# A two-layer graph network on Trainium2: comparisons on 2-byte operands, and another split between two passes

## What is computed

```
h = relu(layernorm(x))
agg = segment_sum(h[src] + edge_attr, dst)            # layer 0
x = x + batchnorm(relu(agg @ W1 + b1) @ W2 + b2)
h = relu(layernorm(x));  dis = rsqrt(degree)          # layer 1
h = relu(segment_sum((h @ W1)[src] * dis[src] * dis[dst], dst) + b1)
h = relu(segment_sum((h @ W2)[src] * dis[src] * dis[dst], dst) + b2)
x = x + (h - mean(h)) / sqrt(var(h) + eps) * ln_w + ln_b
```

## Time and profile before

| | |
|---|---|
| median of 3 runs | 2910.58 us (2907.73 to 2920.95) |
| profiled execution | 2908.32 us, span 2906.8 us |
| busy | PE 2552.8 us (88%), PEld 2416.9, DVE 1743.1 (60%), ACT 888.7, POOL 1993.7 (69%) |
| DMA | 503.37 MB, mean 173 GB/s |

### The profile page before, as it was taken

How to read it: one execution, slowest core, us unless ns; L and a number is a source line. 1 busy time by engine, 2 the same in 40 slices (tenths; PEclk the granted TensorE clock), 3 DMA queues, 4 the chain that set the end, 5 groups by cost and what they waited for, 6 DMA issues and landing times.

```text
span 2906.8 us, 64340 instructions
## 1 busy us (share of the span) xinstructions
PE 2552.8 (88%) x25984; PEld 2416.9 (83%) x25984; DVE 1743.1 (60%) x4148; ACT 888.7 (31%) x1492; POOL 1993.7 (69%) x1903
## 2 busy tenths in 40 slices
PE   0388988989888898895699999999997999999996
PEld 0277878878787787784699999999997999999996
DVE  8898999989988899895444444454430222222222
ACT  7344444444444444454522222232210000000001
POOL 6777777777777778710377777767706777777772
PEclk9899999999999999996799999999998999999998
DMA  4455565555556555543765555655557666666664
GB/s 116 118 149 144 147 171 151 155 157 153 148 160 153 150 148 168 148 125 105 231 204 201 163 200 196 211 181 179 200 186 203 221 206 214 208 213 199 199 214 131
DMA packets 341214, 503.37 MB, mean 173 GB/s; under 512 B 278659, under 2 KB 284217, under 8 KB 316082
## 3 DMA queue, kind: packets, MB, share of 16 engines
q1 hardware_dynamic: 280102, 402.60, 42.8%
q0 software_dynamic: 60192, 93.34, 14.0%
q10 hardware_dynamic: 616, 3.20, 0.4%
HBM read 361.86 MB, written 137.13 MB: 172 GB/s over the span
## 4 chain that ended last, share of the span: by engine, by line
PE 42%; POOL 37%; issue 11%; DVE 5%; DMA 2%; ACT 1%; SPq 1%; DVEq 0%; ACTq 0%; POOLq 0%
POOL arena L1273 37%; PE psum L1110 32%; PE psum L1089 3%; PE psum L1132 3%; PE psum L1071 1%; DMA arena<-table,srcT 1%; ACT arena L818 1%; DMA arena<-in_edge_attr_dram 1%; SPq L1288 0%; PE psum L1125 0%; PE psum L1195 0%; DMA arena<-table 0%; DVE arena L961 0%; DVE arena L834 0%; DVE arena L844 0%
## 5 line engine op out<-in xcount | busy, mean ns | idle before, releaser
L1273 POOL DMA_INDIRECT arena<-table,srcT x1840 | 1913.0, 1040 | 696.3 <-issue 626.5
L1110 PE MATMUL psum<-arena 125*125 125x193 bf16 (+1 forms) x19200 | 2009.1, 250 | 44.8 <-DMA arena<-counts 23.0
L1110 PEld LDWEIGHTS psum<-arena 125*125 125x125 fp8e4 x19200 | 1879.1, 140 | 87.1 <-DMA arena<-counts 23.5
L1211 ACT CAST arena<-psum 125x500 uint16<-125x500 f32 (+1 forms) x923 | 647.3, 711 | 1084.3 <-PE psum L1089 1079.8
L1089 PE MATMUL psum<-arena 128*125 128x300 f16 x1775 | 609.9, 346 | 31.6 <-DVE arena L961 24.5
L961 DVE TENSOR_SCALAR arena<-iota,keyT,oddT 128x300 f16<-128x300 f16 x1775 | 579.3, 353 | 1.4 <-PE psum L1089 1.3
L1089 PEld LDWEIGHTS psum<-arena 128*125 128x125 f16 x1775 | 247.8, 140 | 79.5 <-DVE arena L961 58.4
L971 DVE SCALAR_TENSOR_TENSOR arena<-relT,psum 128x960 bf16<-128x960 f16 x272 | 308.6, 1134 | 0.0
L987 DVE TENSOR_TENSOR arena<-arena 128x650 f32<-128x650 f32 (+1 forms) x334 | 272.8, 817 | 24.8 <-DMA arena<-in_edge_attr_dram 24.6
L958 DVE TENSOR_TENSOR arena<-modT,psum 128x625 f16<-128x625 f16 x355 | 281.0, 792 | 0.2 <-issue 0.2
L994 DVE TENSOR_REDUCE arena<-psum 96x65 f32<-96x195 f32 (+1 forms) x275 | 96.3, 350 | 307.4 <-PE psum L1132 303.4
(11 more groups left out here) (219 smaller groups left out, 954.2 us busy)
## 6 DMA issues: line engine op xcount, KB each, us to landing
arena<-counts SPq DMA_DIRECT2D x121, 1600.0 KB
counts<-arena SPq DMA_DIRECT2D x71, 1600.0 KB, 6.1
arena<-in_edge_attr_dram SPq DMA_DIRECT2D x166, 320.0 KB
arena<-table,srcT POOLq DMA_INDIRECT x1840
table<-arena SPq DMA_DIRECT2D x8, 1050.0 KB
table<-arena SPq DMA_DIRECT2D x25, 168.0 KB
arena<-table SPq DMA_DIRECT2D x4, 1050.0 KB
arena<-in_x_dram ACTq DMA_DIRECT2D x4, 700.0 KB
```

The source lines that it names most:

```text
L1110: last = pe.matmul(ps_v[n % 2][0:PN, 0:xc], A(slot)[0:PN, j, 0:PN], Xs[0:PN, j, 0:xc], start=(j == 0), stop=(j == J - 1))
L1211: act.copy(A2(slot)[0:PN, :, i // 2 * NWORD:i // 2 * NWORD + n_w], ps_b[at % NBANK][0:PN, :].rearrange("p (j x) -> p j x", x=NWORD)[:, :, ...
L1273: pool.indirect_dma_start(out=gbuf(slot)[0:parts, t, :], out_offset=None, in_=tables[k], in_offset=bass.IndirectOffsetOnAxis(ap=idx, axis= ...
```

## The change

Three things. First, `DENSE` becomes (62, 69, 69): pass 0 treats 62 windows as dense and builds 62 tiles, pass 1 builds 9 and loads 60; `QG[0]` goes from 88 to 102. Second, a table of the numbers as 2-byte floats is put in PSUM once, each number five times in a row, and the two comparisons read it; a mask is now made by two `tensor_tensor` operations on 480 columns each instead of one `scalar_tensor_tensor` on 960. Third, for that the layouts turn: `relT` and its source in DRAM have the 10 edges of a partition innermost, a mask has the 10 t of one slot adjacent (so the weights of one t are 96 elements with a step of 10), and `ob` has the 5 runs of one number adjacent (weights: 125 elements with a step of 5).

```diff
-DENSE = (54, 69, 69)
+DENSE = (62, 69, 69)
-        relT = sb("relT", [P, NT, G], F16)
+        relT = sb("relT", [P, G, NT], F16)
+        n_num = (PN * NB4 + 1) // 2
+        ps_n5 = psum[:, 2, P:P + n_num]
+        num_dn = ps_n5.bitcast(F16)[:, 0:PN * NB4].rearrange("p (d n) -> p d n", n=NB4)
         def ob(k):
-            return part(o_ob, k, n_ob).bitcast(F16)[:, 0:NB4 * PN].rearrange("p (n d) -> p n d", d=PN)
+            return part(o_ob, k, n_ob).bitcast(F16)[:, 0:NB4 * PN].rearrange("p (d n) -> p d n", n=NB4)
         def sbuf(n):
+            return part(o_S, n, NT * W // 2).bitcast(BF16).rearrange("p (w t) -> p w t", t=NT)
...
+            nums = arena[:, o_t + NE + 16:o_t + NE + 16 + n_num]
+            V(dve.memset(nums, 0.0))
+            V(dve.tensor_copy(nums.bitcast(F16)[:, 0:PN * NB4].rearrange("p (d n) -> p d n", n=NB4),
+                              iota[:, 0:PN].rearrange("p (d a) -> p d a", a=1).broadcast_to([P, PN, NB4])))
+            V(dve.tensor_copy(ps_n5, nums))
...
-                        mod = modT[:, v:v + NB4].rearrange("p (n a) -> p n a", a=1).broadcast_to([P, NB4, PN])
-                        it = ps_i[:, 0:PN].rearrange("p (a d) -> p a d", a=1).broadcast_to([P, NB4, PN])
-                        dve.tensor_tensor(ob(four % NOB), mod, it, ALU.is_equal)
+                        mod = modT[:, v:v + NB4].rearrange("p (a n) -> p a n", a=1).broadcast_to([P, PN, NB4])
+                        dve.tensor_tensor(ob(four % NOB), mod, num_dn, ALU.is_equal)
...
-                        rel = relT[:, :, g:g + 1].broadcast_to([P, NT, W])
-                        it = ps_i[:, 0:W].rearrange("p (a w) -> p a w", a=1).broadcast_to([P, NT, W])
-                        dve.scalar_tensor_tensor(out=S, in0=rel, scalar=0.0, in1=it, op0=ALU.add,
-                                                 op1=ALU.is_equal).then_inc(v_S, 1)
+                        for t0 in (0, NB4):
+                            rel = relT[:, g:g + 1, t0:t0 + NB4].broadcast_to([P, W, NB4])
+                            last = dve.tensor_tensor(S[:, :, t0:t0 + NB4], rel, num_dn[:, 0:W, :], ALU.is_equal)
+                        last.then_inc(v_S, 1)
...
-                    pe.matmul(to[:, :, 2 * side:2 * side + 3], ob(v // NB4 % NOB)[:, v % NB4, :],
+                    pe.matmul(to[:, :, 2 * side:2 * side + 3], ob(v // NB4 % NOB)[:, :, v % NB4],
...
-                            last = pe.matmul(ps_q, S[0:parts, t, :], e3(v % NEDGE)[0:parts, t, :, :],
+                            last = pe.matmul(ps_q, S[0:parts, :, t], e3(v % NEDGE)[0:parts, t, :, :],
```

More of the change, by code:

```diff
@@ L13 @@
 U16 = mybir.dt.uint16
-U8 = mybir.dt.uint8
 X = mybir.AxisListType.X
@@ L310, in bass_gnn_preln_kernel @@
         ps_i = psum[:, 2, 0:P]
+        n_num = (PN * NB4 + 1) // 2
+        ps_n5 = psum[:, 2, P:P + n_num]
+        num_dn = ps_n5.bitcast(F16)[:, 0:PN * NB4].rearrange("p (d n) -> p d n", n=NB4)
+        assert NT == 2 * NB4
         ps_t = [psum[:, i, :] for i in range(2)]
@@ L346, in sbuf, with sbuf_rows @@
         def sbuf(n):
+            return part(o_S, n, NT * W // 2).bitcast(BF16).rearrange("p (w t) -> p w t", t=NT)
+        def sbuf_rows(n):
             return part(o_S, n, NT * W // 2).bitcast(BF16).rearrange("p (t w) -> p t w", w=W)
@@ L514, in sp_load @@
             sp.dma_start(run_first, row_first).then_inc(l_first, 16)
-            sp.dma_start(dst_i, dst_turned.rearrange("p t g -> p (t g)")).then_inc(l_dst, 16)
+            sp.dma_start(dst_i, dst_turned.rearrange("p g t -> p (g t)")).then_inc(l_dst, 16)
             sp.dma_start(base_b, group_first.broadcast_to([P, NG])).then_inc(l_dst, 16)
@@ L728, in dve_lists @@
             dve.wait_ge(l_dst, 2 * 16)
-            firsts = base_b[:, 0:G].rearrange("p (a g) -> p a g", a=1).broadcast_to([P, NT, G])
-            dve.tensor_tensor(relT[:, :, :], dst_i.rearrange("p (t g) -> p t g", g=G), firsts, ALU.subtract).then_inc(
+            firsts = base_b[:, 0:G].rearrange("p (g a) -> p g a", a=1).broadcast_to([P, G, NT])
+            dve.tensor_tensor(relT[:, :, :], dst_i.rearrange("p (g t) -> p g t", t=NT), firsts, ALU.subtract).then_inc(
                 v_list, 1)
@@ L738, in dve_check_lists @@
         def dve_check_lists():
-            every = relT.rearrange("p t g -> p (t g)")
+            every = relT.rearrange("p g t -> p (g t)")
             dve.wait_ge(v_list, 2)
@@ L968, in dve_pass @@
                     if g < G:
-                        rel = relT[:, :, g:g + 1].broadcast_to([P, NT, W])
-                        it = ps_i[:, 0:W].rearrange("p (a w) -> p a w", a=1).broadcast_to([P, NT, W])
-                        dve.scalar_tensor_tensor(out=S, in0=rel, scalar=0.0, in1=it, op0=ALU.add,
-                                                 op1=ALU.is_equal).then_inc(v_S, 1)
-                    else:
-                        rel = relh_l[0:R, :].rearrange("p (t a) -> p t a", a=1).broadcast_to([R, 2, W])
-                        it = ps_i[0:R, 0:W].rearrange("p (a w) -> p a w", a=1).broadcast_to([R, 2, W])
-                        dve.scalar_tensor_tensor(out=S[0:R, 0:2, :], in0=rel, scalar=0.0, in1=it, op0=ALU.add,
-                                                 op1=ALU.is_equal).then_inc(v_S, 1)
+                        for t0 in (0, NB4):
+                            rel = relT[:, g:g + 1, t0:t0 + NB4].broadcast_to([P, W, NB4])
+                            last = dve.tensor_tensor(S[:, :, t0:t0 + NB4], rel, num_dn[:, 0:W, :], ALU.is_equal)
+                        last.then_inc(v_S, 1)
+                    else:
+                        rel = relh_l[0:R, :].rearrange("p (a t) -> p a t", a=1).broadcast_to([R, W, 2])
+                        dve.tensor_tensor(S[0:R, :, 0:2], rel, num_dn[0:R, 0:W, 0:2], ALU.is_equal).then_inc(v_S, 1)
                 elif kind in ("rest1", "rest2"):
@@ L1131, in pe_pass @@
                         for t in range(nt):
-                            last = pe.matmul(to, S[0:parts, t, :],
+                            last = pe.matmul(to, S[0:parts, :, t],
                                              gbuf(slot)[0:parts, t, :].rearrange("p (s f) -> p s f", s=3),
@@ L1420, in slow_group @@
             pool.sem_clear(t_idx)
-            gb, S = gbuf(0), sbuf(0)
+            gb, S = gbuf(0), sbuf_rows(0)
             for t in range(nt):
@@ L1982 @@
     laid['x'] = x.reshape(-1, PN, F).transpose(1, 0, 2).reshape(PN, -1)
-    for name, a in (('src_turned', src), ('dst_turned', dst)):
-        laid[name] = a[0:n_groups * P * NT].reshape(n_groups, P, NT).transpose(1, 2, 0)
+    for name, a, order in (('src_turned', src, (1, 2, 0)), ('dst_turned', dst, (1, 0, 2))):
+        laid[name] = a[0:n_groups * P * NT].reshape(n_groups, P, NT).transpose(*order)
     behind = _np.stack([_np.full(P, n_nodes, dst.dtype), _np.zeros(P, dst.dtype)], axis=1)
```

## The result

The changed kernel takes 3178.31 us (median of 4 runs, 3175.94 to 3181.82) against 2914.76 before (2907.73 to 2920.95): ratio 1.091, 95% interval 1.087 to 1.094. It is slower by 9%; forecast were 2857 us, and a range that ended at 2975. The profiled execution took 3180.1 us, its span is 3178.8.

The account below looks back on a forecast made before the run. Pass 0 was held bound by POOL's gathers while pairs last, then by DVE with PE close behind; passes 1 and 2 kept PE busy. Gains of 23 and 31.5 less 1.5 make 53: 2910.6 to 2857 us, range 2810 to 2975.

Parts of the forecast that it names:

- Part 3: Side effects: stepped weight loads in all passes taken as free, and 1.5 us more in the prologue.
- Below twice it gives nothing: Weight loads: the slower-strided-weights rival costs no time while the load's time per column is under twice the old.
- up to twice the time per column costs nothing, and I take nothing: Weight loads: hidden under the matmul before, 85 ns against about 43 in the columns, so cost set to zero.
- The rival: Strided weights slower: loads outlast their covering matmuls in all passes; +238 us, 3095 at four times; chance 0.18 above three times.
- Part 1: The split 62 and 9: pass 0 gains 23 us and pass 1 31.5, pass 2 nothing.
- The eight added tiles are no wait of their own: Pass 0: the added tiles' builds, evictions and 1.6 MB stores were taken as covered by the step's gain of 23 us.
- 14.43 us a pair: Pass 0: POOL's pace for one gathered group plus one without a gather; 65 pairs take 938 us instead of 1140.
- 6.4 a group behind: Pass 0 after the pairs: 28 added groups at 6.4 us each, bounded by 6.1 and 7.3, 179 us.
- The working sums of a pair: Pass 0: PE 13.1 and DVE 12.1 us per pair, both below 14.43, so POOL keeps the pace.
- Part 2: DVE comparisons: five builds' numbers 0.395 us, a mask 0.64, buying no time while POOL leads but letting groups behind run at 6.4.
- gathers are relieved: Pass 0: if shorter DVE comparisons shorten gathers, pairs fall to PE's pace, 65 us more saved, 2792; chance 0.10.

Follow-up runs that it names:

- act62: pairs62 with the stores of finished tiles issued by ACT on its own queue instead of SP's; 2844 us, ratio 0.974 to the kernel before.
- adjacent_read: The changed kernel with PE reading the same number of weights from the same buffers as adjacent rows, so sums are of other numbers; 2936 us.
- act54: pairs54 with the stores of finished tiles on ACT's queue; 2869 us, ratio 0.983 to the kernel before.
- pairs form: Comparisons with keys copied twice side by side, weights adjacent, one operation a mask, against the old form; 0.565 us alone for 960 columns, against 1.07.
- pairs54: The kernel before, at its split of 54 tiles, with keys copied twice for faster comparisons and weights left adjacent; 2866 us, ratio 0.983.
- short54: pairs54 with the second rest operation of a group cut from 650 columns to 65, so less DVE work; 2826 us, ratio 0.969.
- noload: pairs62 with edge features loaded only for the first two groups and reused in all others; 2843 us, ratio 0.975 to the kernel before.
- wait62: act62 with SP still waiting for each tile's last eviction where it had issued the store; 2912 us, ratio 0.998 to the kernel before.
- pairs62: The same comparisons and adjacent weights as pairs54, with the split at 62 tiles; 2920 us, ratio 1.001 to the kernel before.
- masks62: The changed kernel with builds as before (adjacent weights, old comparison), masks still stepped; 3145 us, ratio 1.079 to the kernel before.

## Why the prediction was wrong

In runs, taken in this order, the miss of 321 us is 3178 - 2936 = 243 for the stepped weights, 2936 - 2920 = 15 for the comparison in halves, 2920 - 2844 = 76 for the wait in SP's order, less 13 by which act62 is faster than the 2857 of the forecast.

**Part 3 failed: "Below twice it gives nothing" was right, "up to twice the time per column costs nothing, and I take nothing" was a guess.** The load has 3.7 times the time in its columns. The rival said four times, 0.172 us a mask, +238 us and 3095; measured are 0.167 and 243. Its mechanism and its size were right, with a chance of 0.18, and by passes too: after loses 163, 55 and 21 us against adjacent_read, where the rival had 150, 52 and 36. Its 3095 is short of 3178 by what part 1 had wrong. Only the build was under-sized (0.028 for 0.055). An unmeasured price with bounds of 0 and 238 us should not have been set to its lower end because the engine has cover. The Trainium skill, "Advanced Engine Details and Errata", section "Memory Cachelines", had spoken against the change. Its 16-byte lines fit the loops above: nothing at steps of up to 6 bytes, the full price from 16 on. Its rule that two hits in a line are enough does not quite: a step of 8 bytes hits each line twice and costs 8%.

**Part 1 failed, first in one sentence: "The eight added tiles are no wait of their own: their builds, evictions and stores (1.6 MB each) are in this step."** Their bytes were counted, but not what stands behind the store on SP's queue, though the front text says that every engine takes its instructions in order. The terms that hung on it were 14.43 us a pair and 6.4 a group behind. The stretches of act62, where the queue is clear:

```profile
105.00:1297.00 1192.00, 1113.45 (x10386) 1013.02 (x10384) 1034.73 (x3120) 614.89 (x948) 722.05 (x642) 0.99 0.56 161
1375.00:2110.00 735.00, 730.98 (x8170) 723.07 (x8170) 227.99 (x781) 135.39 (x213) 508.54 (x532) 1.00 0.62 205
2128.00:2825.00 697.00, 663.39 (x7705) 658.90 (x7705) 122.08 (x404) 20.09 (x75) 502.82 (x532) 0.98 0.62 201
```

Its gathers run from 106.2 to 1022.7, 14.1 us for each of 65, and 273 us follow to the last add at 1296.1, where before there were 81: 192 for 28 groups, 6.9 each (forecast 6.4). Pass 0 ends 32 us earlier than in the earlier trace rows (forecast 23), pass 1 takes 33 less by the stretches (forecast 31.5; 768 to 735), and pass 2 gains nothing.

That looks like the forecast, and 2844 is near its 2857, but for pass 0 it is luck. act54 has the same comparisons and the same queues as act62 and differs from it in the split alone. The last adds of pass 0, in act54 and in act62:

```profile
1289.58 0.28 DVE L1066 SCALAR_TENSOR_TENSOR acc<-psum,acc 64x125 f32<-64x125 f32 x1
```
```profile
1296.10 0.28 DVE L1066 SCALAR_TENSOR_TENSOR acc<-psum,acc 64x125 f32<-64x125 f32 x1
```

So the split makes pass 0 not 23 us shorter but 7 longer, even with the queue clear: a pair of act54 takes 13.9 us, not 14.43, so there is less to remove, and the groups behind take 6.9, not 6.4. Pass 1 takes 35 us less, from last add to last add, and the 25 us that the split brings in runs are all from there. Pass 0 is shorter than before by the faster comparisons, 39 us at 54 tiles, of which the forecast had nothing. The working sums of a pair were near: PE 13.1 and DVE 12.1 of 14.1 us are 93% and 86%, and act62 has PE busy for 93% and DVE for 87% of pass 0. (1587 steps are 0.380 tile a group, not 0.377, which moves a pair by 0.04 us.)

**Part 2: mis-sized, and it mattered little.** Numbers 0.45 us (forecast 0.395), a mask 0.94 (0.64). The pairs form comes to the forecast's values, 0.39 and 0.56 + 0.08 for the keys' copy, but the forecast had them for another form. For the numbers the Trainium skill's "VectorE: DVE Perf Modes", in the later section "Why PSUM operands drop a tier" that caps PSUM operands at two per cycle, was nearer than the tier table; what decides, by L178 against L174, is whether the innermost run of the operands is two adjacent elements or one repeated.

**The rival "gathers are relieved" held in part.** Gathers of pass 0 from 105 to 1015 us (busy, mean ns), in pairs54 and then in short54, which differ only in DVE's work:

```profile
L1312 POOL DMA_INDIRECT arena<-table,srcT x645 | 711.3, 1103 | 207.7 <-issue 195.4 <-PE psum L726 11.4 <-PE psum L1164 0.9
```
```profile
L1313 POOL DMA_INDIRECT arena<-table,srcT x669 | 704.7, 1053 | 214.9 <-issue 202.3 <-PE psum L726 11.4 <-PE psum L1165 1.2
```

The kernel before has 1147 in this stretch (1155 over all of pass 0). Nothing of POOL was changed. With 50 ns less in each of 780 gathers short54 gains 40 us (2866 to 2826, ratio 0.969 [0.968, 0.971]), more than either theory gave. pairs54 has most of its 49 us from here too: its gathers take 1112 ns over all of pass 0 for 1155, which is 34 us in 780 of them. The forecast had given this a chance of 0.10, because pass 1, with the same comparisons, has short gathers.

## What to carry to other kernels

A layout that makes the writer of a tile faster is paid by its reader: price the reader's step before counting the writer's gain, and where no row has that price, measure it alone first (loops of 40 matmuls did it here). When work is added to a queue that runs in order, list what stands behind each new wait on it: here the stores made edge loads late by their wait, not by their bytes, and busy shares of 90% on PE and 81% on DVE looked like the limit. Taking the loads away without taking work from either engine (noload) told in one run what two cuts of work had not. And where several things change together, compare the final version with one that differs in one of them alone: a total near the forecast had hidden that the split gives nothing in pass 0.

## What the runs showed of the hardware

- 96 weights of 2 bytes: steps 1 to 3 are free under a matmul of 192 columns (0.083 us), step 4 costs 8%, 5 35%, 8 doubles it (0.177), 10 and 12 0.167. About 1.85 ns for each 16 bytes touched where the load sets the pace, an estimate.
- Loads on SP's queue behind its wait for another engine: in wait62 that wait alone costs 67 us of 2912 against act62; the store ahead of the load in the queue costs at most 9 (pairs62 against wait62).
- `tensor_tensor` on 2-byte operands with its table in PSUM: 1.07 us for 960 columns when an operand repeats one element innermost, 0.57 with pairs; writing rows of 5 with gaps of 5 costs 0.50 for 480 columns against 0.36 adjacent.
- A gather on POOL took less time where DVE had less to do beside it: 1147, 1103 and 1053 ns from 105 to 1015 us in before, pairs54 and short54, with DVE busy for 815, 724 and 681 of these 910 us. That it is DVE's work was shown only by the cut in short54. It is not DVE's busy time alone: after has 685 us and 1106 ns, masks62 742 us and 1145 ns. Which part of an operation disturbs a gather was not tried.
